# Attention masks written into the PSUM bank by ScalarE for four key tiles a group, in place of a clearing pass on VectorE for two

## The reference, cut to what matters

```
q, k, v = x @ W.T, split into 16 heads of 16
scores  = (q @ k.T) / 4
scores  = where(mask[None, None, :, :], -inf, scores)     # mask: 512 x 512, the same for all heads and batches
out     = softmax(scores) @ v                              # then @ Wo.T, an RMS norm and a modulation; x = x + that
```

## Time and profile before

| | |
|---|---|
| median of 3 runs | 1181.97 us (1180.37 to 1187.44) |
| span of the profiled execution | 1176.1 us |
| attention, col tiles of groups 0 to 31 | from 43.7 to about 627 us |
| experts and the rest | from 636.87 us to the end |
| TensorE busy | 1132.8 us (96%) |
| VectorE busy | 814.5 us (69%) |
| ScalarE busy | 734.6 us (62%) |
| GpSimd busy | 524.7 us (45%) |

### The profile page before, as it was taken

One profiled execution on the slowest core, in us unless ns is written; L12 is line 12 of the kernel. 1 busy time (PEld: TensorE's weight loads), 2 busy tenths in 40 slices (PEclk: granted clock), 3 DMA queues, 4 the chain that ended last, 5 costly groups with the idle time before them and its releaser, 6 DMA issues.

```text
span 1176.1 us, 23436 instructions
## 1 busy us (share of the span) xinstructions
PE 1132.8 (96%) x7525; PEld 770.1 (65%) x7582; DVE 814.5 (69%) x2327; ACT 734.6 (62%) x1628; POOL 524.7 (45%) x837
## 2 busy tenths in 40 slices
PE   8899999999999999998988999999999999999988
PEld 4333433434334343342426999999999999999968
DVE  5888888787897878978774444346555555677747
ACT  2466667666676766666566656756666565666645
POOL 8324145583764846747471565346223222222220
PEclk8999999999999999999999999999999999999999
DMA  8655637468275572662726596936665765723536
GB/s 219 205 179 185 211 108 227 132 199 247 86 232 187 171 233 87 219 207 97 279 102 223 160 309 217 360 72 175 175 189 157 224 209 153 248 47 67 164 90 215
DMA packets 101616, 213.65 MB, mean 182 GB/s; under 512 B 10917, under 2 KB 71341, under 8 KB 93046
## 3 DMA queue, kind: packets, MB, share of 16 engines
q1 hardware_dynamic: 86038, 192.42, 49.8%
q0 software_dynamic: 14304, 18.69, 8.7%
q10 hardware_dynamic: 1152, 1.05, 0.4%
HBM read 239.28 MB, written 74.29 MB: 267 GB/s over the span
## 4 chain that ended last, share of the span: by engine, by line
PE 43%; POOL 2%; DMA 2%; DVE 2%; issue 1%; ACT 1%; SPq 1%; POOLq 0%; ACTq 0%
PE bank L1080 37%; PE bank L1239 1%; PE bank L1095 1%; DMA x<-yout,rows 1%; PE bank L1109 1%; PE bank L1199 1%; POOL routed L1952 1%; PE bank L1181 1%; DMA routed<-xw,idx 1%; PE bank L1274 0%; PE bank L1219 0%; POOL run L840 0%; DMA w_parts<-in_W 0%; POOL gt L840 0%; DVE tb L840 0%
## 5 line engine op out<-in xcount | busy, mean ns | idle before, releaser
L1615 DVE CUSTOM_DVE_ANT_0 junk<-bank,mneg 128x512 bf16<-128x512 f32 x512 | 335.6, 683 | 92.1 <-PE bank L1151 91.3
L1347 ACT ACTIVATE pt<-bank 128x512 f32<-128x512 f32 x512 | 301.8, 595 | 150.1 <-PE bank L1166 102.7
L1962 POOL DMA_INDIRECT x<-yout,rows x78 | 123.2, 1579 | 287.3 <-ACT yout L1425 242.7
L1080 PE MATMUL bank<-hid,w 128*128 128x256 f32 x1872 | 243.5, 287 | 3.8 <-DVE hid L1763 3.8
L1080 PEld LDWEIGHTS bank<-hid,w 128*128 128x128 f32 x1872 | 230.1, 191 | 5.7 <-issue 4.3
L1763 DVE TENSOR_TENSOR hid<-full,hid 128x256 fp32r<-128x256 f32 x312 | 132.3, 427 | 142.3 <-ACT full L1420 140.9
L1415 ACT ACTIVATE hid<-bank,biases 128x256 fp32r<-128x256 f32 x312 | 149.3, 479 | 96.1 <-PE bank L1080 94.7
L1166 PE MATMUL bank<-mneg,identb 128*128 128x512 bf16 x391 | 148.7, 380 | 0.0
L1420 ACT ACTIVATE full<-bank,biases 128x256 f32<-128x256 f32 x312 | 148.4, 476 | 0.0
L1080 PE MATMUL bank<-rowsT,w 128*128 128x256 f32 x936 | 123.0, 285 | 1.2 <-issue 1.2
L1181 PE MATMUL bank<-pt,vaug 128*17 128x512 f32 x1024 | 123.2, 599 | 0.7
(11 more groups left out here) (183 smaller groups left out, 1463.8 us busy)
## 6 DMA issues: line engine op xcount, KB each, us to landing
w<-split_weights SPq DMA_DIRECT2D x80, 1024.0 KB
w<-split_weights SPq DMA_DIRECT2D x40, 2048.0 KB
split_weights<-w_parts SPq DMA_DIRECT2D x64, 512.0 KB, 3.8
w_parts<-in_W SPq DMA_DIRECT2D x64, 256.0 KB, 4.5
split_parts<-parts SPq DMA_DIRECT2D x28, 384.0 KB, 2.6
rows<-routed SPq DMA_DIRECT2D x39, 258.0 KB, 3.6
stacks<-split_parts SPq DMA_DIRECT2D x36, 256.0 KB, 5.2
qst<-split_parts SPq DMA_DIRECT2D x24, 256.0 KB, 5.0
```

The lines of the kernel that those rows point to most:

```text
L1080: product = T.matmul(ps, w[p], x[q], start=(k == 0 and n == 0), stop=(k == len(weights) - 1 and n == 2))
L1347: A.activation(pt[n % len(pt)][:, :], bank[3 + n % 2][:, :], ACT.Exp, scale=float(D) ** -0.5).then_inc(exped.sem, 1)
L1615: V.tensor_tensor_reduce(junk[n % 2][:, :], bank[n % 3][:, :], mneg[:, 0, st, :], 1.0, FLOOR, ALU.add, ALU.max, rowmax[gi % 2][:, hh, st:s ...
L1962: G.indirect_dma_start(x2_dram, bass.IndirectOffsetOnAxis(ap=rows[j % NS][:, tt, E + 1:E + 2].bitcast(U32), axis=0), yout[j % NY][:, tt], ...
```

## The change

Of the 16 col tiles of each group from group 1 on, four, `(0, 3)`, `(1, 0)`, `(2, 3)` and `(3, 0)`, are now **seeded**: right after the exponential of the tile two before, ScalarE copies `mneg[:, 1, kt]` into the same bank (a new instruction on L1360 of the new program, 128 x 512, bf16 to float32, behind a wait for that exponential's own end). The col product of the tile waits for the copy instead of the exponential, starts without overwriting, and so adds the scores to the mask. It has no mask product. The other twelve tiles of the group, the two formerly cleared ones among them, have a mask product. VectorE clears no tile from group 1 on. Group 0 is as before (two clears, 14 mask products). For 31 groups this makes 124 copies more on ScalarE, 62 clears fewer on VectorE and 62 mask products fewer on TensorE (386 for 448).

```diff
+SEEDED_HEADS = (3,), (0,), (3,), (0,)
...
-                    if k % 2 == 0 and n == 2:
+                    if i == 2 and k % 2 == 0 and n == 2:
                         out.append(("clear", i - 2, k, 0))
...
+    seeded = signal("seeded", [(gi, kt, hh) for gi, kt, hh in cols_at if gi and hh in SEEDED_HEADS[kt]])
...
-        queue.wait_ge(*cleared.at((LAST_GROUP, 2, 0)))
...
                 ps = bank[3 + n % 2]
-                pe.wait_ge(*(exped.at(cols_at[n - 2]) if n >= 2 else v_ready.at((0, ST - 1))))
+                seed = (gi, kt, hh) in seeded.value
+                if seed:
+                    pe.wait_ge(*seeded.at((gi, kt, hh)))
+                else:
+                    pe.wait_ge(*(exped.at(cols_at[n - 2]) if n >= 2 else v_ready.at((0, ST - 1))))
...
-                limit = (gi, kt, hh) in cleared.value
+                limit = seed or (gi, kt, hh) in cleared.value
...
-                                   start=True, stop=limit)
+                                   start=not seed, stop=limit, skip_group_check=seed)
...
-                if kt % 2 == 0:
+                if (gi, kt, 0) in cleared.value:
                     pe.wait_ge(*cleared.at((gi, kt, 0)))
...
                 A.activation(pt[n % len(pt)][:, :], bank[3 + n % 2][:, :], ACT.Exp, scale=float(D) ** -0.5).then_inc(exped.sem, 1)
+                after = cols_at[n + 2] if n + 2 < len(cols_at) else None
+                if after in seeded.value:
+                    act.wait_ge(masks_made, MASKS)
+                    act.wait_ge(*exped.at((gi, kt, hh)))
+                    A.activation(bank[3 + n % 2][:, :], mneg[:, 1, after[1], :], ACT.Copy).then_inc(seeded.sem, 1)
```

## The result

| | before | changed |
|---|---|---|
| median of the runs shown with the result | 1181.33 us (4 runs) | 1165.63 us (4 runs) |
| ratio of the runs | | 0.984, 95% interval 0.980 to 0.988 |
| span of the profiled execution | 1176.1 us | 1162.1 us |

The forecast was 1169 us. The change is faster by 1.6%, or 15.7 us between the medians, 14.0 between the spans. The forecast had 13.1 (11.6 and 1.5).

A forecast was written before the change was run, and what follows sets the result against it. TensorE's full queue was taken as the bound from 60.6 to 530.8 us. The span of 1176.1 less 11.6 and 1.5 gave 1163 us, plus 5.9 made 1169 us; range 1162 to 1179 us.

The forecast's parts named there:

- TensorE's slots: From 60.6 to 530.8 and 560.3 to 588 us: one mask product fewer per weighing, 0.218 us each; -11.6 us.
- The bank's turn: Col products reusing a bank: 0.19 us won or 0.20 us lost at each weighing, taken as equal; 0.
- VectorE's relief: 62 clears leave VectorE's queue; half of the 3.2 us TensorE waited for VectorE is saved; -1.5 us.
- The copies: On ScalarE under the weighing: 0.62 us each, hidden with 0.4 us to spare; 0, at most +8 us.
- GpSimd's stretches: 530.84 to 560.3 and 588 to 636.87 us: GpSimd, scatter or weights limit; TensorE's 2.0 us saved isn't passed on.
- Rival D: At the weighings ScalarE becomes the bound, from 0.95 us a copy on; 1207 us with copies of 1.2; chance 0.1.
- the 623 to 626: Sign in the profile after: the experts' first product starts at 623 to 626 us instead of 636.87.
- The 5.9 us around the span: Whole kernel: the median of the runs lies 5.9 us above the profiled span, added to 1163 us.
- A: The forecast itself: TensorE's slots decide; 1165 to 1173 us; chance 0.5.
- C: All 62 products and VectorE's relief are passed on, GpSimd's stretches included; 1164 us and below; chance 0.1.
- B: At the weighings TensorE's waits for ScalarE eat most of the gain, 0.15 us each; 1176 us; chance 0.2.
- E: Further stretches at 1.2 GHz where TensorE waits for GpSimd, 1.7 us each; with two, 1174 us; chance 0.1.

The follow-up runs named there:

- e1: The changed kernel without seeds: all 16 col tiles from group 1 on have a mask product, no clears; 1180.85 us, ratio 0.9998 to before.
- e5: The changed kernel without seeds, tiles (0, 0) and (2, 0) of groups 1 to 31 with neither clear nor mask product; 1176.81 us, ratio 0.994 to before.
- e3: The changed kernel with each of the 124 copies made twice; 1180.75 us, ratio 1.0005 to the kernel before.
- e6: The changed kernel with tiles (1, 1), (1, 2), (3, 1), (3, 2) seeded instead, so copies come behind the weighing; 1233.14 us, ratio 1.041 to before.
- e4: The change made in groups 1 to 25 alone, groups 26 to 31 as before; 1166.27 us, ratio 0.988 to the kernel before.
- e8: The change made in groups 26 to 31 alone, the earlier groups as before; 1183.38 us, ratio 0.999 to the kernel before.
- e12: The changed kernel with only the first of the two seeds at each weighing, no clears; 1170.01 us, ratio 0.992 to the kernel before.
- e11: The changed kernel run a second time, nothing altered; 1168.44 us, ratio 0.987 to the kernel before.
- e7: The changed kernel with tiles (1, 1) and (3, 1) seeded as well, six seeds a group; 1184.38 us, ratio 1.001 to the kernel before.

## Why the prediction was right

**TensorE's slots, -11.6 us: the sum was right, its parts weren't.** I counted one slot net at each weighing, four out and two in, 1.74 us a batch. The parts by e1, e5 and the change: four seeds save 0.80, 0.87, 0.79, 0.47 us by kind, 2.92 us for 3.49 by slots. The two products that replace the clears cost 0.29, 0.44, 0.34, 0.19, 1.25 together, for 1.74. Seeds less products are 1.7 us a batch. The bank's turn takes from both, and I had put its two effects as equal. They nearly are, 0.57 against 0.50 us a batch. I had assumed that and not derived it, so the zero of this term is in part luck.

**VectorE's relief, -1.5 us: shown, and larger.** It is 0.44 us a batch (e5), all in the groups where the norm's scaling stands in VectorE's queue, and 2.6 us from group 1 to group 26 in e5's trace. e5's whole time gives 4 to 11 us, which that doesn't explain. TensorE's listed waits fell by only 1.4 us, since most of the single waits are too short for that view.

**The copies, 0: right.** 602 ns for my 620, hand-overs of 0.03 us for my 0.05, 0.66 us of idle time left for my 0.4, mostly because the hand-overs are shorter. Rival D put the limit at copies of 0.95 us. e3 with 1.2 us ended level with before, 15 us above the change by the medians. D's formula gave +38 us for that length, since it let TensorE notice every late exponential. e6 is D in another place.

**GpSimd's stretches: open in effect, partly wrong in reason.** The wait of VectorE for GpSimd of the earlier trace rows is still there, in the changed kernel's timeline of VectorE, 13.2 us earlier:

```profile
542.21 0.79 DVE L1677 SCALAR_TENSOR_TENSOR osb<-osb,ssq,gain_shift 128x256 f32<-128x256 f32 x1 [0.62 <-POOL ssq L845]
```

That stretch moves with the lead gained before it. The last one is different. There I had taken GpSimd, scatter and weights for the limit, but at 636.87 us TensorE had waited for them by a mere 1.04 us. In the changed kernel that wait is gone, and the chain runs over exponentials, squares and copies. The same product starts at 621.99 us, before the 623 to 626 that I had named as a sign. How much of the saving in groups 26 to 31 is passed on stays open (e4, e8).

**The 5.9 us around the span: wrong.** The profiled execution of the changed kernel took 1163.8 us for a span of 1162.1, so 1.7 us lie around it. The executions of before that ran beside the experiments have 1.7 to 1.8 us too. So the rest of my 5.9 was the difference between one execution and the median, and 1163 + 1.7 would have been nearer the profiled execution, and the median, 1165.6, lies between.

**Rivals.** A came true, at its lower end. C's 1164 us was nearer to the median than A's middle, and no run excludes it: VectorE's relief was larger than forecast, and e8's interval leaves room for all of the last groups' products. B is out, with 3.3 us of waits where it needed 8. Its mechanism is there (the 0.20 us of e12), but it takes 0.57 us a batch, 0.07 us a weighing, where B had 0.15. E's second dip didn't come in the profiled execution: the clock fell once there, for 3.4 us, as in before. In e11, the same kernel, it didn't fall there at all, and in e8 for 6.8 us and then for 3.4, so it belongs to the scatter.

## What to carry to other kernels

Work moved to an engine that is idle for a third of the time is free only where that engine waits for something long: here 124 copies gained 1.3 to 1.6% before each weighing and lost 4% behind it. Where two banks take turns, price a step by the whole turn (product, mask, exponential, hand-over) beside the sum of slots. A product then costs its slot only where other work stands in the same turn. And when the whole time scatters, compare the median length of the repeated unit between two traces: it told 0.1 us apart where the medians of several runs couldn't tell 3. It shows where a change acts, while the total still has to be measured, as e1 shows.

## What the runs showed that I had not expected

**The scatter has a place.** Windows at the same time in the changed kernel's two profiled executions, first the one shown above, then e11's (columns as in the earlier trace rows, the clock third from the end):

```profile
43.50:50.30 6.80, 6.80 (x35) 3.53 (x34) 6.75 (x23) 5.43 (x10) 4.00 (x4) 1.00 0.88 282
```

```profile
43.50:50.30 6.80, 6.36 (x16) 3.09 (x17) 5.05 (x17) 2.39 (x4) 4.70 (x4) 0.50 0.88 273
688.60:692.00 3.40, 3.40 (x15) 3.04 (x14) 1.16 (x2) 1.92 (x5) 2.52 (x3) 0.51 1.01 299
784.20:787.60 3.40, 3.40 (x18) 3.40 (x18) 2.20 (x8) 2.17 (x6) 2.76 (x3) 0.50 0.77 257
```

In e11 TensorE ran at 1.2 GHz for 6.8 us more near 43 us, right behind the start-up in which it waits for VectorE, and group 1 began 3.7 us later (63.6 for 59.9 us). From 36 to 43.5 us TensorE had been busy for 5.14 us in e11 and for 4.92 in the other, both at full clock. What decides between the two isn't shown. Such a stretch, of 3.4 or 6.8 us, is in nine of the 14 profiled executions, in kernels with and without the change, and in one of the two executions of the change and of e7's kernel, so it isn't the change's. Two more, of 3.4 us each, fell into the experts' products of e11, whose part took 548.8 us for 543.1. They can have cost 3.4 us of that. With the same instructions in the list, the span was 1169.4 us for 1162.1.
